# Fusing the attention matmul steps of each key block into one TensorE step, in a macaron transformer layer on eight cores

## What is computed

```python
q = (x @ Wq.T + bq).reshape(b, l, h, hd).transpose(0, 2, 1, 3)   # h = 32 heads of hd = 128
k, v = ...                                                       # the same with Wk, Wv
scores = jnp.einsum('bhqd,bhkd->bhqk', q, k) / math.sqrt(hd)
scores = jnp.where(causal, scores, -jnp.inf)
att = jax.nn.softmax(scores, axis=-1)
out = jnp.einsum('bhqk,bhkd->bhqd', att, v)
return out.transpose(0, 2, 1, 3).reshape(b, l, d) @ Wo.T + bo

x = x + 0.5 * ffn(layernorm(x))
x = x + attn(layernorm(x))
x = x + 0.5 * ffn(layernorm(x))
```

## Time and profile before

| | us |
|---|---|
| runs of the kernel before | 7004.98 and 7815.08 (median 7410.03) |
| profiled execution | 7013.42 |
| its span (slowest core) | 7011.7 |
| spans of the 8 cores | 6966.3 to 7011.7 |

### The profile page before, as it was taken

One profiled execution on the slowest core, in us unless ns is written; L12 is line 12 of the kernel. 1 busy time (PEld: TensorE's weight loads), 2 busy tenths in 40 slices (PEclk: granted clock), 3 DMA queues, 4 the chain that ended last, 5 costly groups with the idle time before them and its releaser, 6 DMA issues.

```text
span 7011.7 us, 67133 instructions; the slowest of 8 cores (6966.3 to 7011.7 us)
## 1 busy us (share of the span) xinstructions
PE 6011.9 (86%) x23920; PEld 1980.8 (28%) x23920; DVE 1199.0 (17%) x2064; ACT 1100.0 (16%) x1575; POOL 241.2 (3%) x464
## 2 busy tenths in 40 slices
PE   4567899999899999899999899999998798898983
PEld 1202333333233333333333333323332233232320
DVE  3341111111111111111111111111111011101024
ACT  0000222222222222222222222222222000000000
POOL 0000000000000000000000000000000011111100
PEclk8658999999999999999999999999998799999985
DMA  6001211111211111211111211111110333333304
GB/s 103 2 0 30 40 28 34 28 34 28 40 28 34 28 34 28 40 28 34 28 34 28 40 28 34 28 34 28 37 38 4 110 108 130 110 126 114 124 31 193
DMA packets 71235, 356.06 MB, mean 51 GB/s; under 512 B 13584, under 2 KB 29968, under 8 KB 39056
## 3 DMA queue, kind: packets, MB, share of 16 engines
q0 software_dynamic: 43280, 301.44, 17.9%
q1 hardware_dynamic: 27648, 50.34, 2.0%
HBM read 454.94 MB, written 83.89 MB: 77 GB/s over the span
## 4 chain that ended last, share of the span: by engine, by line
PE 82%; issue 6%; DVE 5%; DMA 4%; ACT 2%; DVEq 0%; ACTq 0%; POOL 0%; POOLq 0%; SPq 0%
PE psA L701 14%; PE psB L704 10%; PE psA L702 9%; PE psB L703 9%; PE psA L902 7%; PE psB L902 7%; PE psE L811 5%; PE psE L800 4%; PE psC L762 4%; PE psC L676 4%; PE psC L329 2%; DMA RT<-xh 2%; DMA out_hbm<-BIG 1%; PE psC L331 1%; DVE BIG L730 1%
## 5 line engine op out<-in xcount | busy, mean ns | idle before, releaser
L781 ACT ACTIVATE BIG<-psC,ct 128x512 bf16<-128x512 f32 (+3 forms) x1280 | 912.0, 713 | 3402.5 <-PE psE L811 2171.9
L701 PE MATMUL psA<-RT,BIG 128*128 128x512 bf16 x3072 | 1168.5, 380 | 159.3 <-DVE BIG L730 2.0
L704 PE MATMUL psB<-RT,BIG 128*128 128x512 bf16 x3072 | 1165.5, 379 | 0.0
L703 PE MATMUL psB<-RT,BIG 128*128 128x512 bf16 x3072 | 1164.6, 379 | 0.0
L702 PE MATMUL psA<-RT,BIG 128*128 128x512 bf16 x3072 | 1164.4, 379 | 0.0
L790 DVE TENSOR_TENSOR BIG<-BIG,mpad 128x128 bf16<-128x128 bf16 (+3 forms) x512 | 166.0, 324 | 3304.8 <-ACT BIG L781 3303.4
L701 PEld LDWEIGHTS psA<-RT,BIG 128*128 128x128 bf16 x3072 | 293.8, 96 | 1331.6 <-issue 1327.0
L800 PE MATMUL psE<-BIG 128*128 128x512 bf16 x1280 | 516.2, 403 | 86.7 <-DVE BIG L837 63.5
L762 PE MATMUL psC<-BIG 128*128 128x512 bf16 (+3 forms) x1280 | 457.8, 358 | 117.7 <-ACT BIG L781 111.6
L902 PE MATMUL psA<-BIG 128*128 128x512 bf16 x2048 | 488.7, 381 | 56.2 <-DMA BIG<-wo_hbm 20.2
L902 PE MATMUL psB<-BIG 128*128 128x512 bf16 x2048 | 486.7, 380 | 39.5 <-DMA BIG<-av_hbm 10.7
(11 more groups left out here) (169 smaller groups left out, 2940.0 us busy)
## 6 DMA issues: line engine op xcount, KB each, us to landing
BIG<-wo_hbm POOLq DMA_DIRECT2D x125, 1024.0 KB, 5.2
BIG<-wqkv POOLq DMA_DIRECT2D x96, 1024.0 KB, 8.2
wo_hbm<-wo_a POOLq DMA_DIRECT2D x32, 1024.0 KB, 12.0
out_hbm<-BIG SPq DMA_DIRECT2D x64, 512.0 KB, 2.8
RT<-xh POOLq DMA_DIRECT2D x4, 4096.0 KB, 29.1
av_hbm<-BIG SPq DMA_DIRECT2D x128, 128.0 KB, 2.7
BIG<-av_hbm POOLq DMA_DIRECT2D x16, 1024.0 KB, 9.0
boj<-bo_a POOLq DMA_DIRECT2D x125, 0.2 KB, 4.8
```

The lines of the kernel that those rows point to most:

```text
L701: t.matmul(psA[:, 0:512], wch, RTs(c, 0, 512), start=(c == 0), stop=False)
L703: t.matmul(psB[:, 0:512], wch, RTs(c, 1024, 512), start=(c == 0), stop=False)
L704: return t.matmul(psB[:, 512:1024], wch, RTs(c, 1536, 512), start=(c == 0), stop=False)
L781: lambda s: s.activation(Psb[par][:, rs:512], psC[:, 0:w], AF.Exp, bias=ct_eb, scale=ct_es),
```

## The change

In the loop over the chunks of a query block, the three TensorE steps of a chunk (scores of chunk c+1, AV of chunk c, and for odd c the sums of chunks c-1 and c) are replaced by one step with the same matmuls in the same order. Exp and mask steps stay as they are, and so do the score steps that begin a query block. The fused step carries the waits of all its parts ahead of its first matmul, and one increment on its last; psC's lower half, psE0 and psE1 get the same certificate. The attention list of a head has 104 tasks in place of 160, and `emit_interleaved` deals them over the same 124 projection tasks.

```diff
-                if c + 1 < nch:
-                    attn_t.append(lambda m4=m4, c=c: smm_step(m4, c + 1))
-
-                def savst(c=c, par=par, m4=m4, nch=nch, vH=vH, bvH=bvH):
-                    def sav(t):
-                        return t.matmul(psE0[:, :], vH[:, 128 * c:128 * (c + 1)],
-                                        Psb[par][:, :], start=(c == 0), stop=(c == nch - 1))
-                    p.step("tensor", sav, reads=[bP[par], bvH], writes=[bE0])
-                attn_t.append(savst)
-                if c % 2 == 1 or c == nch - 1:
-                    cpair = [c - 1, c] if c % 2 == 1 else [c]
-
-                    def sumst(cpair=cpair, nch=nch):
-                        def summ(t):
-                            mm = None
+                cpair = ([c - 1, c] if c % 2 == 1 else [c]) \
+                    if (c % 2 == 1 or c == nch - 1) else None
+
+                def fusedst(c=c, par=par, m4=m4, nch=nch, cpair=cpair,
+                            vH=vH, bvH=bvH, qT=qT, kT=kT, bqT=bqT, bkT=bkT):
+                    has_smm = c + 1 < nch
+                    reads = [bP[par], bvH, cstM]
+                    writes = [bE0]
+                    if has_smm:
+                        w1 = 512 - 128 * max(0, c + 1 - 4 * m4)
+                        reads += [bkT, bqT]
+                        writes += [bClo]
+                    if cpair is not None:
+                        reads += [bP[cc % 2] for cc in cpair]
+                        writes += [bE1]
+
+                    def body(t):
+                        if has_smm:
+                            t.matmul(psC[:, 0:w1], kT[:, 128 * (c + 1):128 * (c + 2)],
+                                     qT[:, 512 * m4 + 512 - w1: 512 * (m4 + 1)],
+                                     start=True, stop=True)
+                        mm = t.matmul(psE0[:, :], vH[:, 128 * c:128 * (c + 1)],
+                                      Psb[par][:, :], start=(c == 0), stop=(c == nch - 1))
+                        if cpair is not None:
                             for cc in cpair:
                                 mm = t.matmul(psE1[0:1, :], ones_c[:, :], Psb[cc % 2][:, :],
                                               start=(cc == 0), stop=(cc == nch - 1))
-                            return mm
-                        p.step("tensor", summ,
-                               reads=[bP[cc % 2] for cc in cpair] + [cstM], writes=[bE1])
-                    attn_t.append(sumst)
+                        return mm
+                    p.step("tensor", body, reads=reads, writes=writes)
+                attn_t.append(fusedst)
```

## The result

The changed kernel took 7135.5 us (median of 11 runs), the kernel before 7012.1 us (median of 10). The ratio is 1.0172, with a 95% interval of 1.016 to 1.0184. So it is slower by 1.7%, some 120 us, where the prediction had 57 us (7070). The time lies inside the stated range and the loss is under 2%, but it is clear of the measurement's noise and 2.1 times what the prediction had added up.

A forecast was written before the change was run, and what follows sets the result against it. TensorE's own queue was taken to set the time. Gaps +6.4 and borders -5.1 us a head gave +40 us over 31 heads; with +16 for the last head, 7013.4 became 7069, say 7070 us, range 6985 to 7160.

The forecast's parts named there:

- The hidden cost: Between two bare projection steps (P, four matmuls each): 0.31 us waiting for TensorE's own last write, hidden by one short step.
- the count of gaps: 93 gaps a head between projection steps: bare ones from 31 to 57, +6.4 us a head.
- The borders: Three passages between projections (q to k, k to v, v to next q): shorter by 5.1 us a head.
- the 0.3 I gave back: At the v border: gain in the borders cut from 5.4 to 5.1 us a head, by choice.
- the walk: Step-by-step timing of the borders in the new order: 7.2 (q to k), 7.7 (k to v), 14.3 us (v to q).
- three P or more: Projection steps before a fused step of a masked diagonal chunk, said to cover exp and mask: cost 0.
- The last head: Final head's attention, running alone: later exps and fused steps waiting for mask or normalisation, +16 us, bounds 8 and 24.
- The rule on semaphores: TensorE increments serialize at about 26 ns each; 56 fewer a head would give 45 us less than the sum.
- the clock at k to v: Rival: the clock drops at the k to v border too, 3.8 us a head, 7188 us; chance 0.10.
- the rival with better borders: Shorter v border keeps the clock at 2.4 GHz, 3.1 us a head, 6974 us; chance 0.11.
- Scores exposed to a late exp inside the gaps: Rival: 40 fused steps a head wait for ACT, 0.1 us each, 7194 us; chance 0.05.
- fewer steps pay: Rival: each of 56 steps saved a head gives something, 2.8 us a head, 6983 us; chance 0.06.

The follow-up runs named there:

- e3: Kernel before the change, with TensorE steps no longer waiting for TensorE's own semaphore; ratio 0.9113 to the kernel before, 6389 us.
- e4: Changed kernel, with TensorE steps no longer waiting for TensorE's own semaphore; ratio 0.9009 to the kernel before, 6314 us.
- e1: Changed kernel with its dealing kept, but score, AV and sums issued as three steps again; ratio 1.0101 to the kernel before, profiled 7059 us.
- e5: Changed kernel's dealing, score, AV and sums as three steps, no TensorE waits for its own semaphore; 6249 us profiled, 6268 us when repeated.

## Why the prediction failed, point by point

- **The hidden cost and the count of gaps** held. 57 bare pairs, 1.29 and 1.91 us, 122.5 us a head as predicted; before 116.4 against 116.1. The term is +6.1, predicted +6.4. That exp stays covered inside a projection held too, and e3 and e4 show the mechanism of the 0.31 us by taking it away.
- **The borders** were the step that failed: predicted -5.1 us a head, measured -2.9 (34.3 to 31.4). The q border was right. Most of the miss is at v, for two reasons. I took the border of one head, 16.42 us, for all; the mean of 31 is 15.87, and the 0.3 I gave back was too little. And the walk ends at the first P of q, without the wait behind it: the prediction gave masked chunks "three P or more" and a cost of 0, but the first fused step behind this border has a single P before it, and its mask stands on DVE behind the column sums' three steps. It waits 1.27 us in the mean (gap 2.51 in place of 1.24). In e1, with the steps split, 0.88 of this is left: about a third belongs to the fusing, the rest to the order. At k the walk was 0.7 short: the median border is 7.39, as I had it (7.35), but the mean is 7.9, since in the first 6 of the 31 heads the column sums there run near the low level (3.2 to 3.6 us for eight, in the other 25 heads 1.9), and the wait behind it is 0.5 in place of 0.35. The old border was 0.25 longer than the one I read, so 0.5 of the miss is there. Together it is 2.2 us a head, 70 us.
- **The last head** was mis-sized: +24.9 in place of +16 (+23.1 by the medians of the cores). The exp that waits for the AV was right (+0.42). Of the 7 us missing by the medians, 3.6 are the own wait in 33 hand-overs to a fused score, 0.11 each: from ACT it took 0.25 in place of 0.14 us, from the mask 0.36. Another 0.8 are exps behind sums, 16 times 0.15 in place of 0.10. e4 shows that the first is the own wait; the rest of the 7 is not assigned.
- **The rule on semaphores**: e5 and e4 have the same order and no own waits, and e5 has 56 increments a head more. In both, P, score, AV, P takes 1.295 us in the median and with sums 1.913, so no cost of an increment shows here. The estimate from the Trainium skill's page "TensorE: Matmul & The Clock Gate", section "The cost: per-tile semaphore tail", of 45 us less than my sum, does not agree with these rows; that section measures small tiles packed into the array, and none stand here.
- **The rivals**: the clock at k to v went the other way. Before, the column sums behind k took 3.0 to 3.6 us in all 31 heads; after, only in the first 6. At v the column sums still ran near the low level (2.5 to 3.5 us), so the rival with better borders fell too. Scores exposed to a late exp inside the gaps did not come: scores wait for ACT 10 us in 31 heads. That fewer steps pay did not come true with own waits. Without them the changed kernel is the faster one, but e5 shows that the new order made that gain, and that fusing still cost 46 to 65 us of it.
- **The sum and the chances**: its own bounds, -2 and -8 at the borders, give 7166 and 6980 us with the +16, and not the 7150 and 6990 that it states. The 0.84 for "within 2%" came true with a measured 1.7%. But the forecast of 57 us was a difference: a sure loss of 6.4 us a head, less a gain of 5.1 that was much less sure and read mainly off one head.

What stays open is why the clock drops at the first 6 k borders and not at the others, and what the borders would cost with masks and evictions in another order on DVE; that was not tried.

## What to carry to other kernels

Before merging steps, look at what is hidden between steps: a planner that lets an engine wait for its own semaphore leaves a hole behind every step that writes the buffer of the one before (here 0.31 us behind a projection step, and all own waits of TensorE together 9% of the kernel), and small separate steps fill such holes for nothing. Take the own waits out first, on an engine whose steps need no wait for each other; only TensorE was tried here. The same merge that lost 1.7% with them was 1.2% faster without them, through the order that came with it. And a merged step waits for the latest input of all its parts and passes on the earliest output last: where nothing else covers the chain, as in a last head alone, split steps are better.

## What was not expected of the hardware

A wait that is met already still takes time when it stands in the queue behind one that is not: ACT to TensorE took 0.25 us with one own wait behind the wait for ACT, and 0.14 without it. From the mask to a fused score it was 0.36 us with two waits behind (TensorE's own and ACT's) and 0.25 with one: 0.11 us for each. Putting such waits ahead of the one that is met last would save this too; that was not tried.

In e3 and e4 four matmuls of P were issued in 0.86 to 0.87 us, the median on each of the eight cores. The granted clock in stretches of 1000 us of the head loop was 0.93 to 0.97 in e3 and 0.96 in e4, against 0.95 to 0.96 before: the denser work did not lower the clock in these executions.
